# A selective-scan decoder layer on one core: the softplus of channel blocks 4 to 7 is computed inside the scan stage, and the projection to B, C and dt is turned round

## The reference

```
xz = in_proj_weight @ hidden                       # 2048 channels x 512 tokens: x and z
x  = silu(causal depthwise conv, 4 taps, of x)     # u, 1024 channels = 8 blocks of 128
x_dbl = x_proj_weight @ x                          # 160 rows: dt (128), B (16), C (16)
delta = softplus(dt_proj_weight @ dt + dt_proj_bias)
h_t = h_{t-1} * exp(delta_t * A) + delta_t * u_t * B_t      # 16 states per channel, over 512 tokens
y_t = sum_n h_t[n] * C_t[n] + u_t * D
out = out_proj_weight @ (y * silu(z))
```

## Time and profile before

| | us |
|---|---|
| three runs | 1700.11, 1702.56 (median), 1709.99 |
| the profiled execution | 1698.6 |
| its span in the profile | 1696.8 |
| PE busy in the span | 1445.6 (85%) |
| DVE busy | 1349.2 (80%) |
| POOL busy | 1065.7 (63%) |
| ACT busy | 798.0 (47%) |
| mean granted TensorE clock | 0.931 of full speed |

### The profile page before, as it was taken

One profiled execution on the slowest core, in us unless ns is written; L12 is line 12 of the kernel. 1 busy time (PEld: TensorE's weight loads), 2 busy tenths in 40 slices (PEclk: granted clock), 3 DMA queues, 4 the chain that ended last, 5 costly groups with the idle time before them and its releaser, 6 DMA issues.

```text
span 1696.8 us, 19403 instructions
## 1 busy us (share of the span) xinstructions
PE 1445.6 (85%) x5408; PEld 830.0 (49%) x5416; DVE 1349.2 (80%) x2215; ACT 798.0 (47%) x1368; POOL 1065.7 (63%) x684
## 2 busy tenths in 40 slices
PE   7867678999699899999699899999699999836994
PEld 3323223444465565444465565444465665325783
DVE  3488999676899999796899999796899999784212
ACT  3575454245734565245734565245734565222141
POOL 0299999101999899500999899500999999422101
PEclk9988899999699999999699999999699999967997
DMA  3550000412535674513535674512534774600984
GB/s 111 207 204 25 0 0 1 161 38 76 220 121 182 198 242 150 204 44 101 217 124 174 205 238 154 204 44 101 217 125 147 236 233 130 248 25 8 353 333 143
DMA packets 94074, 252.14 MB, mean 149 GB/s; under 512 B 11024, under 2 KB 11152, under 8 KB 88848
## 3 DMA queue, kind: packets, MB, share of 16 engines
q1 hardware_dynamic: 86688, 229.93, 39.9%
q0 software_dynamic: 5120, 16.78, 3.0%
q10 hardware_dynamic: 2160, 4.19, 0.6%
HBM read 207.87 MB, written 42.99 MB: 148 GB/s over the span
## 4 chain that ended last, share of the span: by engine, by line
PE 52%; DVE 18%; issue 13%; POOL 7%; ACT 7%; DMA 2%; DVEq 0%; POOLq 0%; SPq 0%; ACTq 0%
PE bank L1902 10%; PE bank L1780 6%; DVE bank L1253 6%; PE bank L2028 5%; PE bank L1795 4%; PE bank L1834 4%; PE bank L1839 4%; POOL work L659 4%; PE bank L1931 3%; PE bank L1828 3%; PE bank L1923 2%; PE bank L1803 2%; DVE work L1265 2%; PE bank L1802 2%; DVE pairs L1265 2%
## 5 line engine op out<-in xcount | busy, mean ns | idle before, releaser
L659 POOL TENSOR_TENSOR work<-du,BB 128x1024 f32<-128x1024 f32 x255 | 603.0, 2378 | 5.2 <-DVE work L1529 4.4
L926 ACT ACTIVATE bank<-delta,A_sb 128x512 f32<-128x512 f32 x512 | 349.9, 690 | 477.3 <-DVE pairs L1265 260.8
L1253 DVE TENSOR_TENSOR_SCAN bank<-bank,work 128x512 f32<-128x512 f32 x432 | 522.5, 1219 | 12.9 <-ACT bank L926 9.2
L1902 PEld LDWEIGHTS bank<-x3T,ew_up 128*128 128x128 f32 x1488 | 221.1, 196 | 74.5 <-issue 63.2
L1902 PE MATMUL bank<-x3T,ew_up 128*128 128x128 f32 (+1 forms) x1488 | 243.3, 310 | 5.2 <-issue 5.2
L1265 DVE TENSOR_TENSOR pairs<-bank,CB 128x512 f32<-128x512 f32 x240 | 160.9, 671 | 1.6 <-PE bank L1839 0.6
L604 POOL TENSOR_TENSOR col<-col,halfpow 128x4 f32<-128x4 f32 (+1 forms) x8 | 7.8, 973 | 209.8 <-DVE col L1405 209.8
L1265 DVE TENSOR_TENSOR work<-bank,CB 128x512 f32<-128x512 f32 x192 | 128.3, 668 | 0.0
L1795 PE MATMUL bank<-xT,wst 128*128 128x512 f32 x256 | 117.7, 604 | 8.4 <-ACT delta L873 6.6
L1834 PE MATMUL bank<-pairs,ident 128*128 128x512 f32 x160 | 90.6, 650 | 34.4 <-DVE zg L1273 18.8
L2028 PE MATMUL bank<-wst,zg 128*128 128x512 f32 x256 | 117.0, 593 | 0.9 <-DVE zg L1273 0.9
(11 more groups left out here) (243 smaller groups left out, 2518.2 us busy)
## 6 DMA issues: line engine op xcount, KB each, us to landing
ew_up<-in_exp_w SPq DMA_DIRECT2D x93, 512.0 KB, 3.8
ew_dn<-in_exp_w SPq DMA_DIRECT2D x93, 256.0 KB, 4.3
hm<-xs_dram SPq DMA_DIRECT2D x69, 256.0 KB, 4.6
ys_dram<-x3T SPq DMA_DIRECT2D x69, 256.0 KB, 4.5
wst<-in_w_in SPq DMA_DIRECT2D x64, 256.0 KB, 2.7
BB<-bc_dram SPq DMA_DIRECT2D x16, 1024.0 KB, 7.2
CB<-bc_dram SPq DMA_DIRECT2D x16, 1024.0 KB, 9.1
wst<-in_out_w SPq DMA_DIRECT2D x32, 256.0 KB, 2.9
```

What stands on the lines that cost most here:

```text
L659: nc.gpsimd.tensor_tensor(dBu[:, k % CHUNK_SLOTS, :, :], du[:, j % 2:j % 2 + 1, :].broadcast_to([P, 2, T]), BB[:, n0:n0 + 2, :], ALU.mult) ...
L926: nc.scalar.activation(R[q % RING][:, :], delta[:, j, :], ACT.Exp, scale=A_sb[:, j, n:n + 1]).then_inc(S["da_ready"], 1)
L1253: V.tensor_tensor_scan(prod[c % (2 * PAIR_SLOTS)] if on_pool(q) else R[q % RING][:, :], R[q % RING][:, :], dBu[:, c // 2 % CHUNK_SLOTS, c ...
L1902: ins = mm(gu_bank(v)[:, part * n:(part + 1) * n], w[:, part * D + k * P:part * D + (k + 1) * P], rhs, start=(k == 0), stop=(k == KD - 1))
```

## The change

1. **Softplus of blocks 4 to 7** of batches 1 to 3 leaves the gap. In the gap ACT only copies the argument to SBUF (`raw`). Inside the scan stage, |v|, exp, relu, 1 + e (now on ACT), ln and exp(-ln) are put at steps of ACT's list, `lost` and the error at steps of DVE's, the sum and the subtraction at steps of POOL's, blocks 4 and 5 first, 6 and 7 later. Their buffers are those of xT, so the stage's first products wait only for the errors of blocks 0 to 3, one each.
2. **The gap is reordered.** POOL's `norm` for the router comes after `chunk(0)`, three errors and `chunk(1)`; the subtractions of blocks 1 to 3 move into the stage (k = 2, 3, 4). `row_norm` is split into halves at steps 1 and 2 of ACT's list, `x3` goes to step 3. On PE and ACT the `z` and `dl` blocks change places with parts of the quantized layers.
3. **B, C, dt by token tiles.** u is held still, 128 tokens at a time, and all 160 columns of `xpw` are streamed; four matmuls of 160 columns per block. The result has tokens on the partitions; ACT copies it out (`tok_copy`) and PE turns it with eight transposes (`bc_turn`), after which ACT copies dt and B, C as before.
4. One slot for the skip diagonal instead of two, and small tensors and semaphores merged.

```diff
+LATE_LN_AT = {4: 14, 5: 14, 6: 40, 7: 40}
+LATE_SUM_AT = {4: 8, 5: 9, 6: 21, 7: 22}
...
         def sp_e(a, m):
+            if a > 0 and m >= 4:
+                return xT[:, 2 * (m % 2), :]
...
             def chunk(b, k):
                 if k == 2 and b > 0:
-                    pool.wait_ge(S["sum_ready"], NBLK * (b + 1))
+                    pool.wait_ge(S["sum_ready"], NBLK * b + 4)
...
             def phase1(a, m):
                     for i in range(4):
                         softplus_sum(a, i)
-                    for i in range(4):
-                        softplus_lost(a, i)
+                    softplus_lost(a, 0)
                     softplus_less(a, 0)
                     du_block(a, 0)
                     chunk(a, 0)
                     for i in range(1, 4):
-                        softplus_less(a, i)
+                        softplus_lost(a, i)
+                    chunk(a, 1)
                 if m is not None:
                     norm(2 * m + 1)
-                if a is not None:
-                    for i in range(4, 8):
-                        softplus_sum(a, i)
...
-                        if k > 0:
+                        if k > (0 if b == 0 else 1):
                             chunk(b, k)
-                        if k == 1 and b > 0:
-                            for i in range(4, 8):
-                                softplus_less(b, i)
+                        if b > 0:
+                            for i in range(1, NBLK):
+                                if LATE_LESS_AT[i] == k:
+                                    softplus_less(b, i)
+                                if i >= 4 and LATE_SUM_AT[i] == k:
+                                    softplus_sum(b, i)
...
+            def raw(a, m):
+                sc.wait_ge(S["dl_ps"], NBLK * a + m + 1)
+                nc.scalar.activation(delta[:, m, :], dl_bank(a, m)[:, :], ACT.Identity, bias=dtb[:, m:m + 1]
+                                     ).then_inc(S["raw_ready"], 1)
...
             def product(c):
-                    if c == 0 and b > 0:
-                        ve.wait_ge(S["sp_err_ready"], NBLK * (b + 1))
-                    if 4 <= c < 8 and b > 0:
-                        ve.wait_ge(S["delta_ready"], NBLK * b + c + 1)
+                    if c < 4 and b > 0:
+                        ve.wait_ge(S["sp_err_ready"], NBLK * b + c + 1)
+                    elif c < 8 and b > 0:
+                        ve.wait_ge(S["delta_ready"], NBLK * b + c - 3)
...
             def bc_dt(a, k):
                 pe.wait_ge(S["u_ready"], NBLK * a + k + 1)
-                bc = mm(bank[4][0:2 * NS, :], xpw[:, k, DTR:DTR + 2 * NS], u[:, k, :], start=(k == 0), stop=(k == NBLK - 1))
-                dt = mm(bank[5][:, :], xpw[:, k, 0:DTR], u[:, k, :], start=(k == 0), stop=(k == NBLK - 1))
+                for t in range(TT):
+                    dst = bank[4][:, t * CBD:(t + 1) * CBD] if t < 3 else bank[5][:, 0:CBD]
+                    ins = mm(dst, u[:, k, t * P:(t + 1) * P], xpw[:, k, :], start=(k == 0 and t in (0, 3)),
+                             stop=(k == NBLK - 1 and t in (2, 3)))
...
+            def bc_turn(a):
+                pe.wait_ge(S["tok_ready"], 2 * (a + 1))
+                for t in range(TT):
+                    ins = nc.tensor.transpose(bank[5][:, t * P:(t + 1) * P], tok[:, t, 0:DTR], ident[:])
+                ins.then_inc(S["dt_ps"], 1)
+                for t in range(TT):
+                    ins = nc.tensor.transpose(bank[4][0:2 * NS, t * P:(t + 1) * P], tok[:, t, DTR:CBD], ident[:])
+                ins.then_inc(S["bcT_ps"], 1)
```

More of the change, by code:

```diff
@@ L190, in build @@
         hm = sb("hm", [P, 2, T])
-        st = sb("st", [P, TT, 6])
         mv = sb("mv", [P, TT, 2])
-        rstd = sb("rstd", [P, TT])
-        shift = sb("shift", [P, TT])
-        row_shift = sb("row_shift", [P, TT])
+        few = sb("few", [P, 4, TT])
+        rstd, shift, row_shift, sg = (few[:, i, :] for i in range(4))
         col = sb("col", [P, 9, 4])
@@ L326, in build @@
         late_in = [sem(f"late_in{i}") for i in range(LATE_RING)]
-        late_xs_in = [sem(f"late_xs_in{i}") for i in range(LATE_ROWS)]
+        tile_in = [sem(f"tile_in{i}") for i in range(LATE_ROWS)]
         late_ys_out = [sem(f"late_ys_out{i}") for i in range(LATE_ROWS)]
@@ L987, in y_rows @@
                     nc.scalar.copy(ys[n % 2], down_ps[1][:, :]).then_inc(S["y_ready"], 1)
-                if experts:
-                    for i in range(KD if scan else KD // 2):
+                if not scan:
+                    for i in range(KD // 2):
                         x3(i)
@@ L996, in scan_stage @@
                         skip(p // NS)
+                    if scan and experts:
+                        if p in (ROW_NORM_AT, ROW_NORM_AT + 1):
+                            row_norm(b - 1, 2 * b - 1, p - ROW_NORM_AT)
+                        if p == X3_AT:
+                            for i in range(KD):
+                                x3(i)
+                        for m in range(4, NBLK):
+                            if p == LATE_ABS_AT[m]:
+                                late_abs(b, m)
+                            if p == LATE_EXP_AT[m]:
+                                exps(b, (m,))
+                            if p == LATE_RELU_AT[m]:
+                                late_relu(b, m)
+                            if p == LATE_MORE_AT[m]:
+                                one_more(b, m)
+                            if p == LATE_LN_AT[m]:
+                                lns(b, (m,))
+                            if p == LATE_INVERSE_AT[m]:
+                                inverses(b, (m,))
                     if scan and b == 0:
@@ L1078, in first @@
                 exps(0, (0,))
-                one_more(0)
+                one_more(0, 0)
                 lns(0, (0,))
@@ L1324, in scan_stage @@
                         scan_unit(p)
-                    if scan and p == 1 and b > 0:
-                        for i in range(4, 8):
-                            softplus(b, i)
+                    if scan and b > 0:
+                        for i in range(4, NBLK):
+                            if p == LATE_LOST_AT[i]:
+                                lost(b, i)
+                            if p == LATE_ERROR_AT[i]:
+                                softplus(b, i)
                     if scan and b == 0:
@@ L1571, in between @@
                 q1.maxima(0)
+                for i in range(4):
+                    one_more(a, i)
                 q1.scale(1)
@@ L1575, in between @@
                 for i in range(4):
-                    one_more(a, i)
+                    lost(a, i)
                 q1.integers(0)
-                for i in range(4):
-                    lost(a, i)
                 q1.integers(1)
@@ L1811, in dl @@
                     pe.wait_ge(S["bc_ready"], a + 1)
+                elif a > 0 and m >= 6:
+                    pe.wait_ge(S["raw_ready"], 4 * (a - 1) + m - 5)
                 elif a > 0:
```

179 lines of the change are left out of this document (108 added, 71 removed).

## The result

The changed kernel takes 1749.47 us (median of four runs, 1747.84 to 1750.43), the kernel before 1704.07 beside it: a ratio of 1.026, 95% interval 1.023 to 1.030. The forecast was 1717 with 1731 as its upper end: the sign is right, the loss more than twice as large.

A forecast was written before the change was run, and what follows sets the result against it. DVE, PE and POOL nearly full in the scan; the gap's chain runs through POOL's norm to the logits. Three batches at 8.1 us more, 24.3, less 6.1: +18.2 on 1698.6, predicting 1717, range 1686 to 1731.

The forecast's parts named there:

- row shift ready: End of the gap, POOL's list: row shift at 819.8 instead of 825.72, 5.9 us earlier (5 to 7).
- logits start, taken by DVE: Gap's end: PE starts the router's logits at 826.2, 8.3 us earlier; DVE gets them at 833.1.
- places: Mark in DVE's work after logits, visits and ranks: can start at 846.1, 10.5 us earlier.
- unit 15: Scan stage of batch 2: unit 15 reached at 858.7, 8.5 us earlier.
- POOL's wait at k = 8: Scan stage: POOL waits 8 us or more before block 4's sum, for its logarithm 2.6 us after unit 15's start.
- `chunk(9)` behind unit 15: POOL's chunk for unit 18, queued behind sum, gate sums and scatter, starts at unit 15 + 6.3 us.
- unit 15 to 32: Scan stretch where POOL has no spare time: 47.0 us instead of 33.9, so 13.1 us lost.
- unit 32: Scan stage of batch 2: 13.1 us lost, 8.5 gained, unit 32 at 905.7, 4.6 us later.
- unit 32 to 56: Later scan stretch holding the second group's softplus: 50.2 us forecast, 3.5 more than before.
- The second rival: PE's clock stays high over logits and first visit, 3.4 us each; about 6 us more per batch, 1699; chance 0.15.
- the second group: Later softplus (ln at step 40, sums at k = 21, 22): wait costs about nothing beyond DVE's own time; 3.5 us.
- The first stage: First stage, PE the chain throughout: new B, C, dt projection gains 6.1 us once, about 1 if loads were not hidden.

The follow-up runs named there:

- neither suspect: Changed kernel with second operand of the eight `lost` and error instructions from PSUM and POOL's sums behind their logarithms; span 1686.2, ratio 0.992.
- the second execution: The changed kernel profiled once more without an edit; span 1742.3 for 1747.5.
- the projection alone: Kernel before plus only the turned B, C, dt projection, softplus staying in the gap; span 1695.6, ratio 0.9964.

## Why the prediction was wrong, by its own steps

Times of batch 2, on the scale of the trace of before: the 13.2 us by which batch 1 ended later are subtracted.

| step | forecast | measured |
|---|---|---|
| row shift ready (825.72 before) | 819.8 | 819.6 |
| logits start, taken by DVE | 826.2, 833.1 | 826.7, 832.4 |
| places | 846.1 | 844.2 |
| unit 15 | 858.7 | 856.1 |
| POOL's wait at k = 8 | 8 or more | 11.9 |
| `chunk(9)` behind unit 15 | 6.3 | 6.5 |
| unit 15 to 32 | 47.0 | 48.8 |
| unit 32 | 905.7 | 904.9 |
| unit 32 to 56 | 50.2 | 60.5 |
| rest of the batch | 0 | 0.6 |

**Right.** The gap, term by term, with the new `bc_dt` (eight instructions start 1.09 us before what follows, forecast 1.10), POOL's list, and the new wait at k = 8. The second rival's condition was half met: from the logits' start to the visit's it took 5.55 us and not 6.84.

**Right in sum only.** Unit 32 came out within 1 us by POOL's strict order. But the forecast said that the hold costs this; the runs say that with the hold gone DVE's port waits keep 5.2 of it (42.7 for 37.5) and with the port waits gone the hold keeps 8.6 (46.1).

**The step that failed** is the second group, where "the wait costs about nothing beyond DVE's own time: four instructions at 1.0" gave 3.5 us. Two things were mis-sized. The `lost` and error instructions were priced from one row of the first stage, 1.20 us, where DVE had asked shortly before a boundary of POOL's list and won it; here four of them took 10.7 us. And the hold at k = 21 was 10.0 us, not nothing (5.9 where DVE does not wait for the port): with the operand from PSUM, taking it away still gives 2.8 us (53.2 to 50.4); with the operand in SBUF, 6.5. With neither suspect the group costs 3.7 us, which is what was forecast for the whole. The step was 10.9, 10.3 and 9.6 us short in the three batches, 31 together; 9 of them were made up ahead of unit 32, mostly in batch 1, and 21.5 are left of the 32 that were missing in all.

**The first stage** was to give 6.1 us once. It starts 4.1 us earlier, and one `lost` of 5.95 us instead of 1.20 and one of 2.33 for 1.11 take it back and more (1.5 us late at its end); in the second execution they did not. That makes 7.6 us of the miss, and by the runs it is partly chance. The stages behind the last scan are 3.4 us longer (241.5 for 238.1; between 238.8 and 244.1 in the other runs, with no order that follows the edits); that stays open.

**What the trace of before could have told.** In it, 14 times a `lost` or error instruction of DVE came while POOL was in a run, and 14 times it got in at the next boundary; the longest of those took 2.52 us, and three of 2.84 to 2.89 stood beside a chunk that nothing followed at once. So a price of up to 2.9 could be read, and 1.0 was too low, but not one of 6.4. The Trainium skill (SBUF — State Buffer, Who interferes with whom) states that a VectorE instruction with two SBUF inputs contends with a GpSimd instruction that reads SBUF. The same page (SBUF: two separate sides) states that the one that starts first keeps the shared pair of ports for its whole instruction while the other blocks. The runs agree with the first (up to 9.3 us with both in SBUF, 0.69 with one in PSUM), and with the second only where DVE won the boundary. As an estimate from that page, one chunk of 2.36 and its own 0.67 would be 3.0 us an instruction at most, 24 a batch; single instructions went up to 9.3.

## What to carry to other kernels

Before a VectorE instruction with two SBUF operands is moved into a stretch where GpSimd works without pause, price it by GpSimd's run up to the next gap, not by its own length, or give it an operand in PSUM. Where the run can't be avoided, let GpSimd wait for that instruction at the very next point of its list: 0.7 us of GpSimd's time bought 5.8 of VectorE's here, and the same wait two chunks (four instructions) further on bought nothing. A wait put into a strictly ordered list costs what is queued behind it, and two such delays can cover each other, so that undoing either alone shows less than its share. Two table loads around a logarithm also hold back the copy that ACT makes next, and with it whoever waits for that copy (2.7 and 3.4 us of DVE's time here, read from the traces and not tested).

## What the runs showed of the hardware that I had not expected

- A VectorE instruction with two SBUF operands that meets a run of GpSimd's can lose one boundary after another: 5.61 us through four instructions, 9.05 through five, up to 9.3 us. Over the fifteen profiles 155 boundaries were won and 124 to 140 lost, depending on whether one counts a boundary within 0.2 us of the request; the kernel before and the projection alone have 14 won and none lost each. All 67 instructions that lost their first boundary got in only where POOL's list paused, for 0.16 us at the least; none of them got in between two instructions back to back. What decides was not found: the distance in time to the start of GpSimd's instruction does not (0.50 us lost, 0.49 won), nor does the program alone (the same one lost and won).
- VectorE did not get in beside a scatter either: an error instruction that came 0.36 us into one (890.28 to 891.29) did not start, and the chunk behind it got in first.
- The switch of ACT's table inside the stage cost its load: 1.28 us, with the ln 1.30 behind the load's start, as the earlier trace rows had it.
